# A graph network kernel on one core: the gathers' waits moved from TensorE's count of sums to VectorE's count of additions

## What is computed

```python
# L0, attention by dot products over the edges, 8 heads of 32
scores = einsum('ehd,ehd->eh', q[src], k[dst]) / sqrt(32)
e = exp(scores - m[dst]);  p = e / z[dst]
out = segment_sum(v[src] * p[:, :, None], dst)
# L1, sums over neighbours in both directions, then a GRU step
agg_in  = segment_sum(xl_in[src],  dst) / max(count, 1)
agg_out = segment_sum(xl_out[dst], src) / max(count, 1)
# L2, one weight matrix for each of 8 edge types
m = segment_sum(hW[edge_type, src], dst) / deg
# L3, attention with a score for each end of an edge, then a norm over all nodes
e = leaky_relu(a_src[src] + a_dst[dst]);  alpha = softmax over dst
out = segment_sum(xh[src] * alpha[:, :, None], dst) + bias
```

## Time and profile before

| | us |
|---|---|
| median of 3 runs | 8852.08 |
| lowest, highest | 8848.3, 8878.25 |
| span of the profiled execution | 8691.5 |
| dot attention, 587 to 2267 | 1680 |
| layer 1, incoming, 2388 to 3732 | 1344 |
| layer 1, outgoing, 3732 to 5035 | 1303 |
| layer 2, 5651 to 6937 | 1286 |
| edge attention, 7049 to 8514 | 1465 |

### The profile page before, as it was taken

One profiled execution on the slowest core, in us unless ns is written; L12 is line 12 of the kernel. 1 busy time (PEld: TensorE's weight loads), 2 busy tenths in 40 slices (PEclk: granted clock), 3 DMA queues, 4 the chain that ended last, 5 costly groups with the idle time before them and its releaser, 6 DMA issues. The chain is left out here.

```text
span 8691.5 us, 96994 instructions
## 1 busy us (share of the span) xinstructions
PE 6954.1 (80%) x30536; PEld 4265.7 (49%) x30536; DVE 5250.2 (60%) x11418; ACT 1233.5 (14%) x2942; POOL 4541.3 (52%) x4616
## 2 busy tenths in 40 slices
PE   1479999999478788888888899978888867777774
PEld 1246666666345444444555444444444445555552
DVE  8778887888846555533343344443333476667667
ACT  0121111211200000000000045500000032222221
POOL 1015454555367767666666611166766536656550
PEclk9999898999789899999999999989999988889887
DMA  0256555666533333343333444433333443334343
GB/s 7 86 191 165 152 164 146 171 167 167 161 89 89 91 88 89 88 111 112 114 114 116 112 151 164 159 97 92 92 92 91 88 141 106 107 107 110 105 103 97
DMA packets 451712, 1019.27 MB, mean 117 GB/s; under 512 B 122952, under 2 KB 212486, under 8 KB 444573
## 3 DMA queue, kind: packets, MB, share of 16 engines
q0 software_dynamic: 240960, 702.53, 30.3%
q1 hardware_dynamic: 210269, 310.65, 10.9%
HBM read 851.98 MB, written 160.61 MB: 117 GB/s over the span
## 5 line engine op out<-in xcount | busy, mean ns | idle before, releaser
L786 PE MATMUL psum<-rows,oh 128*128 128x257 f32 (+2 forms) x7040 | 2285.3, 419 | 651.5 <-issue 293.1
L813 PE MATMUL psum<-ident,ones 128*128 128x512 bf16 x7660 | 2200.4, 396 | 0.0
L786 PEld LDWEIGHTS psum<-rows,oh 128*128 128x128 f32 x7040 | 1350.2, 204 | 1377.0 <-issue 1062.2
L793 DVE TENSOR_TENSOR acc<-acc,psum 128x264 f32 (+2 forms) x2640 | 1107.7, 420 | 1445.3 <-PE psum L786 794.0
L732 POOL DMA_INDIRECT rows<-qv_tab,src_i x880 | 845.4, 961 | 1362.1 <-PE psum L786 605.6
L1276 POOL DMA_INDIRECT rows<-xh_tab,src_i x880 | 872.5, 991 | 691.6 <-PE psum L1356 369.5
L813 PEld LDWEIGHTS psum<-ident,ones 128*128 128x128 bf16 x7660 | 781.9, 102 | 746.4 <-issue 113.9
L751 POOL DMA_INDIRECT rows<-h_tab,src_i x880 | 917.9, 1043 | 415.6 <-issue 241.7
L751 POOL DMA_INDIRECT rows<-h_tab,wts x880 | 862.7, 980 | 452.8 <-issue 228.0
L751 POOL DMA_INDIRECT rows<-hw_tab,rel_i x880 | 878.9, 999 | 405.5 <-issue 238.6
L793 DVE TENSOR_TENSOR kh<-kh,psum 128x257 f32 x880 | 371.6, 422 | 789.7 <-PE psum L786 500.3
(11 more groups left out here) (410 smaller groups left out, 7966.5 us busy)
## 6 DMA issues: line engine op xcount, KB each, us to landing
wts<-hots SPq DMA_DIRECT2D x220, 256.0 KB
hw_tab<-acc SPq DMA_DIRECT2D x50, 1024.0 KB, 4.1
rows<-part_tab SPq DMA_DIRECT2D x50, 512.0 KB, 5.6
hots<-oh SPq DMA_DIRECT2D x74, 256.0 KB, 2.8
rows<-qv_tab,src_i POOLq DMA_INDIRECT x880
rows<-h_tab,src_i POOLq DMA_INDIRECT x880
rows<-h_tab,wts POOLq DMA_INDIRECT x880
rows<-hw_tab,rel_i POOLq DMA_INDIRECT x880
```

The lines of the kernel that those rows point to most:

```text
L786: nc.tensor.matmul(psum[:, banks[b % len(banks)], 0:row.shape[1]], oh[:, b // GROUP, b % GROUP], row, start=True, stop=True).then_inc(agg_ ...
L793: nc.vector.tensor_tensor(to, to, psum[:, banks[b % len(banks)], 0:width], ALU.add).then_inc(acc_done, 1)
L813: nc.tensor.matmul(bank, ones[:, :].bitcast(BF16)[:, 0:P], busy, start=True, stop=True)
```

## The change

In three places GpSimd's wait before a gather names `acc_done` in place of `agg_done`, with the same number. The gather into a buffer is then held until VectorE has added the bank of the buffer's former slot to the running sums, and no longer only until TensorE has summed the slot. No instruction is added, removed or moved on any engine. The waits of TensorE, VectorE and ScalarE stay as they are.

```diff
     def gather(pool, j, b, table, width, index):
 
-        pool.wait_ge(agg_done, prev(j, b, RING))
+        pool.wait_ge(acc_done, prev(j, b, RING))
         nc.gpsimd.indirect_dma_start(rows[:, b, 0:width], None, table,
                                      bass.IndirectOffsetOnAxis(index, 0)).then_inc(ring[b], 16)
...
     def gather_ahead(pool, m, to, table, index):
 
         if m >= HELD and m % AT_ONCE == 0:
-            pool.wait_ge(agg_done, RING + SLOTS + m - HELD + AT_ONCE)
+            pool.wait_ge(acc_done, RING + SLOTS + m - HELD + AT_ONCE)
...
         def on_gpsimd(pool):
             for n in range(SLOTS):
                 if n >= HELD:
-                    pool.wait_ge(agg_done, summed(n - HELD))
+                    pool.wait_ge(acc_done, summed(n - HELD))
```

## The result

The changed kernel takes 9071.5 us (median of 4, 9051.7 to 9096.5) against 8850.2 for the kernel before. The ratio is 1.0241, with a 95% interval of 1.0214 to 1.0267. It is slower, where the prediction had "no change" as the likeliest, 0.35 on slower, and 8780 to 9060 as its range.

A forecast was written before the change was run, and what follows sets the result against it. It took the exchange between TensorE and VectorE to set the ends of the passes, with no engine as the bound. 8691.5 + 3 + 0 + 0 + 17 = 8711.5 us, with 160.6 around it 8872 us; range 8780 to 9060.

The forecast's parts named there:

- The base: Whole program: the profiled span of 8691.5 us plus 160.6 us around it, to which the changes per pass were added.
- short groups: Dot attention: 87 groups of the usual kind, 14.05 us in the trace against 17.09 us for a long one.
- Landing, and the reader of the rows: All passes: only the reader of gathered rows can suffer from later gathers; 3 us in dot attention, 0 elsewhere.
- the 3 in the sum: Dot attention: direct cost of rows landing later, taken as 3 us from a range of 0 to 10.
- The term of 17 us: Dot attention: late counts at the gathers' new places, half way between 34 us lost and nothing.
- The first rival: Dot attention: gathers beside L939 lock in L1107's late release in every group, 264 us more, 9116 us; chance 0.30.
- Edge attention, 0: Edge attention: rows still land in time, with some 8 us left before and more than 3 after; cost 0.
- Layers, 0: Layers 1 and 2: the new wait costs at most 6 us of the 22 to spare; cost 0.
- The second: Dot attention: with the gathers spread otherwise the 23 long groups go, 70 us faster, 8782 us; chance 0.13.
- The third: Whole program: counts are late because GpSimd waits for that semaphore; without them 209 to 580 us faster; chance 0.06.

The follow-up runs named there:

- the second trace: Profile of the kernel before, unchanged and run against itself: 8826.3 against 8824.2 us, ratio 0.9999; its profiled span is 8870.7 us.

## Why the prediction was wrong

**The base.** The sum stood on 8691.5 us of span and 160.6 us "around the program". That was a wrong reading. Every later run has 2 us between span and time. The 160 us were the distance of a short execution, or of a faster chip, from the timed runs. Most of that distance lies in the dot attention (1680 against 1731 to 1769 on the two chips whose median is near 8825) and the edge attention (1465 against 1494 to 1512). It left the forecast as it was, since the two numbers together are the median. But the 87 "short groups" of the dot attention, on which two rivals were priced, were not the usual case: in the second trace L1107 is late only twice.

**Landing, and the reader of the rows.** Right, and beside the point. L1076 waits for 11.7 us in 5 groups where it waited for 8.0 in one, 3.7 us against the 3 in the sum; the edge attention and the layers wait no longer.

**Dot attention, +3 and +17.** The prediction said that the change moves where the gathers lie, that most late counts found in the group may go, and that new ones may come beside the matmuls for the weights. Both happened: L1107 has no late release, L1045 has 118.7 us of them. The sign of the sum was wrong: measured alone, this pass makes the kernel 89 us faster. The term of 17 us charged the new places with half of what the old ones cost and credited nothing for the old ones that go. The old ones, L1089, L1098 and L1107, are VectorE's own instructions. The new one, L1045, is ScalarE's, and VectorE's L1123 waits 78.1 us for it, where it was 16.5. The first rival, a lock at L939, did not come, although the gathers went where it had them: with this pass changed alone, one starts within 0.7 us before L939's end in 105 of 110 groups (16 in the second trace of before), and no count is late. Its reading of one pair of timelines as a rule was false.

**Edge attention, 0.** This is the step that failed most, 211 of the 358 us between the two traces. Measured alone it costs 207 us. The sentence that failed is "the one who can suffer is the reader of the rows": the working asked only whether rows land in time, "some 8 us are left before". The prediction held that a count raised beside gathers comes late, and that the change moves the gathers, and yet counted late counts in the dot attention alone. What it did not read is L1312: the rows of before show L1468 without idle time, but 2.05 us after L1312's end (7387.13 to 7389.18), hidden behind L1516. With the change the last gather of a group starts 2.7 us later (medians 10.6 and 13.3 us after L1468), and the count rises 4.45 us after L1312's end, when VectorE has nothing else to do. It is the kind of loss that the first rival describes, in the other attention and at 1.9 us a group (13.3 to 15.2 us) where the rival had 3.04.

**Layers, 0.** Also read by landing alone (22 us to spare, of which none was used). Measured alone they cost 152 us. The stretches moved by 4.6, 3.3 and 5.9% (3.3, 2.7 and 4.5% against the second trace of before), over the 1% that the prediction named as the mark of its failure, and the "remote" rows of L793 rose by 138 us, where it expected them near 580. "This idle time costs nothing by itself" misled: GpSimd's pauses end with TensorE's or VectorE's counts and so decide when its gathers run, and these delay TensorE's counts. So GpSimd was in the loop though it was busy for only two thirds of the time. Why resuming on an addition is worse than resuming on a sum stays open for the layers.

**The rivals.** The second, with a chance of 0.13, came true for its pass and was outweighed by the others: L1107's "remote" count is 0, the sign that the prediction named for it, and the 89 us are near its 70. The size is in part luck, as it was priced on long groups that the second trace of before does not have. The third, that the counts are late because GpSimd subscribes to them, fell with the first trace: "remote" is still there. The Trainium skill ("VectorE: DVE Perf Modes", The TRN2 errata) warns that high-rate semaphore increments from one engine can deadlock another. No run here did, and of late counts it says nothing; layer 2 without gathers has the higher rate (949 against 1303 us for the same counts) and no late one, so the rate alone is not what delays them here.

## What to carry to other kernels

On a kernel with gathers on GpSimd, a change of when they run has to be priced by what runs beside them and not only by when the rows are needed. A single pair of timelines is no rule for it: here a gather at L1312's end went with late counts in one kernel and with none in another. List, for each stretch, the short matmuls whose counts another engine waits for, and measure from their end to the start of the waiting instruction also where that instruction shows no idle time: the lateness may be there, covered. And take two profiles of the kernel before, or compare its span with the times, before summing against one of them.

One wait in eight can carry a whole change. It was worth trying the waits of a group one by one: in the dot attention slot 3 alone gave 2.0%, where all eight gave 1.1% (on another chip), and slot 2 alone the full loss in the edge attention.

## What the runs showed of the hardware

- Gathers of 32 bytes a row delay TensorE's counts as much as those of 1 KB (1303 us for the pass in each), plain DMAs of 131 KB from SyncE or GpSimd not at all (948 us).
- A gather at a matmul's end does not always make its count late: `edge_ps` rose 0.01 us after L1312 where the gather was the first of a string, and L1107 was never late with a gather at L939's end in 108 of 110 groups.
- A count can be late and leave no idle time: `edge_ps` rose 2.0 us after L1312's end in the kernel before, 0.03 us ahead of L1468.
- For GpSimd an issue took 0.95 us as a gather and 0.54 us as a plain DMA.
- Without gathers layer 2 ran at a granted clock of 1.00, where it had 0.89 to 0.91. The stretches whose waits grew had the lower clock: the edge attention 0.88, 0.80 with the change, 0.72 with one burst a group. There TensorE's matmuls took longer too (L1356 481 ns before, 521 after), so part of the loss lies in them; how much, no run separates.
- The kernel before took 8705, 8795, 8824 and 8826 to 8829 us on four chips. On the first of them single runs went from 8667 to 8788.
